# Low parts of the attention probabilities ahead of the low parts of the queries and keys in GpSimd's order, and a reciprocal inside the rope's products in VectorE's

## The reference

```
x: 4 x 512 x 256, xn = layernorm(x)
q = xn @ Wq (16 heads of 128), k = xn @ Wk, v = xn @ Wv (4 heads each, shared by 4 query heads)
q, k = rope with a scale by position; scores = q k^T / sqrt(128), causal; attn = softmax(scores)
s = (attn @ v) @ Wo
g = silu(MoE(xn)): 16 routed experts of width 176, top 2 by softmax, and a shared one of width 352
out = x + s * g
```

## Time and profile before

| | |
|---|---|
| median of 3 runs | 750.87 us (749.21 to 753.45) |
| the profiled execution | 753.45 us, its span 751.6 us |
| busy TensorE, VectorE, ScalarE, GpSimd | 628.6, 521.0, 498.9, 528.0 us |
| share of the span | 84%, 69%, 66%, 70% |
| mean granted clock of TensorE | 0.958 of full speed |
| rotate_lo on GpSimd, 80 of them | busy 92.2 us, idle ahead of them 100.0 us |
| low_probs on GpSimd, 64 of them | busy 167.2 us, idle ahead of them 3.9 us |

### The profile page before, as it was taken

The page is one execution under the profiler, slowest core; times in us unless marked ns, Lnnn a source line. Parts: engine busy times, 40 slices in busy tenths (PEclk is TensorE's granted clock), DMA queues, the critical chain, the costliest instruction groups (busy, mean ns, idle before and its releaser), DMA issues.

```text
span 751.6 us, 16683 instructions
## 1 busy us (share of the span) xinstructions
PE 628.6 (84%) x4610; PEld 421.9 (56%) x4611; DVE 521.0 (69%) x1555; ACT 498.9 (66%) x1333; POOL 528.0 (70%) x396
## 2 busy tenths in 40 slices
PE   3667849797989999899998999989877699999982
PEld 1244526464556566565665666656555477777761
DVE  5966649767788877888778887788845254333378
ACT  3685546757768787687867878678775665555542
POOL 4565567897886878878888787888988893554410
PEclk9878998999999999999999999999998899999996
DMA  9355973447544545444454444554486774655873
GB/s 301 93 127 120 211 184 64 90 75 166 101 84 87 97 88 103 86 87 92 89 103 90 87 88 89 102 96 89 85 135 169 211 132 87 147 140 135 215 266 106
DMA packets 233016, 92.39 MB, mean 123 GB/s; under 512 B 203316, under 2 KB 226324, under 8 KB 232980
## 3 DMA queue, kind: packets, MB, share of 16 engines
q1 hardware_dynamic: 228868, 81.40, 50.8%
q0 software_dynamic: 3840, 10.52, 4.7%
q10 hardware_dynamic: 272, 0.02, 0.0%
HBM read 24.72 MB, written 18.96 MB: 58 GB/s over the span
## 4 chain that ended last, share of the span: by engine, by line
POOL 41%; issue 27%; PE 16%; DVE 7%; DMA 5%; ACT 2%; SPq 1%; POOLq 1%; DVEq 0%; ACTq 0%
POOL stage L590 15%; POOL arena L574 11%; PE bank L1606 8%; POOL arena L581 6%; PE bank L1636 5%; POOL xs_dram L636 3%; POOL compare L632 2%; DMA stage<-w_down 2%; PE bank L1615 2%; DMA arena<-x 1%; POOL arena L566 1%; DMA ys_dram<-arena,row_u 1%; DMA arena<-ys_dram 1%; DVE s_sb L1333 1%; DVE arena L1148 1%
## 5 line engine op out<-in xcount | busy, mean ns | idle before, releaser
L830 ACT ACTIVATE arena<-bank,nmax 128x384 f32<-128x384 f32 (+2 forms) x320 | 146.8, 474 | 48.1 <-DVE nmax L1163 47.9
L590 POOL TENSOR_TENSOR stage<-arena,stage 128x1280 bf16<-128x1280 f32 x64 | 167.2, 2613 | 3.9 <-ACT stage L850 3.9
L581 POOL TENSOR_TENSOR arena<-arena 128x512 bf16<-128x512 f32 x80 | 92.2, 1159 | 100.0 <-ACT arena L815 99.8
L1458 PE MATMUL bank<-arena 128*128 128x512 f16 (+7 forms) x768 | 119.1, 306 | 22.0 <-POOL arena L581 19.9
L1163 DVE CUSTOM_DVE_ANT_0 bank<-bank,mask_b 128x512 f32<-128x512 f32 (+3 forms) x256 | 118.8, 519 | 17.8 <-issue 17.8
L1427 PE MATMUL bank<-xnT_hi,arena 128*128 (+1 forms) x320 | 114.1, 399 | 14.9 <-DVE arena L1148 9.7
L1472 PE MATMUL bank<-arena 128*128 128x512 f16 (+7 forms) x768 | 115.3, 300 | 0.0
L1498 PE MATMUL bank<-arena 128*128 (+2 forms) x768 | 99.8, 278 | 16.0 <-DVE arena L1154 13.2
L574 POOL TENSOR_TENSOR arena<-arena 128x512 f32<-128x512 f32 x77 | 98.2, 1284 | 10.3 <-DVE arena L1148 10.0
L1458 PEld LDWEIGHTS bank<-arena 128*128 128x128 f16 (+1 forms) x768 | 66.4, 100 | 65.5 <-issue 26.4
L1498 PEld LDWEIGHTS bank<-arena 128*128 (+2 forms) x768 | 75.5, 99 | 42.8 <-issue 17.6
(11 more groups left out here) (149 smaller groups left out, 1208.9 us busy)
## 6 DMA issues: line engine op xcount, KB each, us to landing
xs_dram<-s_sb SPq DMA_DIRECT2D x12, 516.0 KB, 5.0
stage<-w_gate_up SPq DMA_DIRECT2D x16, 352.0 KB
arena<-ys_dram SPq DMA_DIRECT2D x8, 512.0 KB, 8.4
stage<-w_down SPq DMA_DIRECT2D x16, 176.0 KB
stage<-wq SPq DMA_DIRECT2D x4, 512.0 KB, 7.6
stage<-wo SPq DMA_DIRECT2D x4, 512.0 KB, 7.6
arena<-stage SPq DMA_TRANSPOSE x128, 3.4
stage<-x SPq DMA_DIRECT2D x1, 2048.0 KB, 11.3
```

The source lines that it names most:

```text
L581: pool.tensor_tensor(dst, rot_a[buf], hi, ALU.subtract).then_inc(rot_lo, 1)
L590: pool.tensor_tensor(p_lo[par], probs[par], p_hi, ALU.subtract).then_inc(probs_lo, 1)
L830: return act.activation(dst, src, ACT.Exp, scale=-1.0, bias=nmax[:, par, qt:qt + 1], accum_out=rsum[:, par, to:to + 1])
L1458: ins = pe.matmul(score_bank[u][:, col:col + n_k], qT[a][:, j * S + qt * P:j * S + (qt + 1) * P], kT[m][:, 0:n_k], start=(n == 0), stop=(n ...
```

## The change

Nothing is computed otherwise. In GpSimd's order low_probs of a step comes ahead of the step's rotate_lo (in step 2 also ahead of rotate_sum of k), rotate_lo of k moves from step 2 to behind the steps, and behind the steps low_probs of head 4 comes ahead of rotate_lo of q2. In VectorE's rotate_products the reciprocal of a head's sums comes behind the first of the three products instead of behind the third.

```
--- before.py
+++ after.py
@@ -707,6 +707,7 @@
                     if j == 1 and rd.tile() is not None and not rd.last:
                         pool.wait_ge(rows_ready, rd.tile() + 1)
                         rows_low(rd.tile())
+                    low_probs(rd, j + 1)
                     if j == 2 and not rd.last:
                         rotate_sum("k", rd.item("k"))
                     if j == 1 and rd.tile() is not None and not rd.last:
@@ -715,9 +716,6 @@
                         rotate_lo("q3", rd.i * 5 + 5)
                     elif not rd.last:
                         rotate_lo(f"q{j - 1}", rd.rot(f"q{j - 1}"))
-                    if j == 2 and not rd.last:
-                        rotate_lo("k", rd.rot("k"))
-                    low_probs(rd, j + 1)
                     if rd.early and j < 2:
                         weights_lo(W_FIRST + 2 * rd.i + j)
                     if rd.last and j == 0:
@@ -737,11 +735,12 @@
                     if j == 1 and rd.tile() is not None and not rd.last:
                         scatter()
                 if not rd.last:
+                    rotate_lo("k", rd.rot("k"))
                     rotate_sum("q2", rd.item("q2"))
                     if rd.late:
                         shared_lo(1)
+                    low_probs(rd, GH)
                     rotate_lo("q2", rd.rot("q2"))
-                    low_probs(rd, GH)
 
             round_(Round(0, "first"))
             round_(Round(1, "second"))
@@ -1144,10 +1143,10 @@
                     dve.wait_ge(rot_lo, freed)
                 dve.tensor_tensor(rot_a[buf], ps[:], tab[:, cos, :], ALU.mult)
                 half = DH // 2
+                if inverted_head is not None:
+                    invert_sums(*inverted_head)
                 dve.tensor_tensor(rot_b[buf][0:half, :], ps[half:DH, :], tab[half:DH, sin, :], ALU.mult)
                 dve.tensor_tensor(rot_b[buf][half:DH, :], ps[0:half, :], tab[0:half, sin, :], ALU.mult).then_inc(misc_free, 1)
-                if inverted_head is not None:
-                    invert_sums(*inverted_head)
 
             def value_lo(rd):
                 dve.wait_ge(v_hi, rd.i + 1)
```

## The result

The changed kernel takes 777.8 us (median of 4 runs, 776.3 to 781.6); the kernel before took 750.04 beside it. The ratio is 1.037, with a 95% interval of 1.032 to 1.043: slower by 28 us. The range of the prediction held it because it was wide enough for a rival: the likeliest case, A (767, chance 0.57), did not happen, and rival B (778, chance 0.2) did. The profiled execution took 778.42 us with a span of 776.6, 25.0 over the span of before.

The account below looks back on a forecast made before the run. No engine is full; a ring of dependences across engines sets 31.45 us a round. -3.2 us ahead of the loop, +17.0 over eleven periods and +2.5 behind give +16.3: 767.2 us median, range 757 to 780.

Parts of the forecast that it names:

- A: Whole kernel: each loop round grows by 1.55 us with TensorE's clock kept; 767.2 us, chance 0.57.
- rival B: TensorE: wait ahead of head 4's score grows to about 2.4 us, clock falls every round; 778 us, chance 0.2.
- Part 1: GpSimd, step 2: low_probs of head 3 ahead of k's rotations costs 2.6 us a round before head 4's score.
- Part 2: GpSimd, step 1: low_probs of head 2 ahead of rotate_lo of q0 gains 1.0 us a round.
- Part 3: GpSimd, steps 3 and 0: low_probs of heads 4 and 1 earlier gain 0.1 of 0.67 us; q0's late rope eats the rest.
- Part 4: VectorE: the earlier reciprocal waits 1.0 us at q1, about 0.5 at q3 and k; counted 0 a round, to +0.5.
- The clock: TensorE ahead of head 4's score: likeliest forecast kept full clock, as a 2.4 us wait stays under 2.8; fall given 0.2.
- A's ring: Loop: cycle of dependences from one score of head 4 to the next, 33.05 us against 31.45, without a clock fall.
- B's price: Half-speed score takes 3.2 instead of 1.6 us; ScalarE's last unit starts 0.95 later, 12 x 0.95 = 11 us.
- Ahead of the loop: Rounds before the loop: earlier transfers and less idle time outweigh later losses; -3.2 us at rotate_sum of q1, round 3.
- Behind the loop: Round 14, behind the eleven periods: its rotate_lo of k still comes late, +2.5 us.

Follow-up runs that it names:

- part 2 alone: The kernel before with only low_probs of head 2 moved ahead of rotate_lo of q0; 742.7 us, ratio 0.988.
- part 4 alone: The kernel before with only the reciprocal moved behind the first product of each rope; 754.6 us, ratio 1.005.
- part 1 alone: The kernel before with only low_probs of head 3 moved ahead of rotate_sum of k and rotate_lo of q1 and k; 797.2 us, ratio 1.062.
- the filled kernel: The changed kernel with 8 useless matmuls added each round in TensorE's wait ahead of the score of head 4; 768.5 us, ratio 1.023.

## Why the prediction came out as it did

- *Part 1* (low3 ahead of RL k): forecast 7.55 us from RS q1 to the score; measured 354.54 to 361.96, 7.42. Right. Alone it makes the slowest kernel of all, and without it and part 4 the rest is a gain.
- *Part 2*: forecast 3.84 us from P2's end to the scatter's start and 1.0 us of gain; 0.90 alone. Right.
- *Part 3*: forecast 0.1 us of gain because the rope of q0 comes late; 0.06 alone. The first product waits for GpSimd as forecast.
- *Part 4*: forecast a wait of 1.0 us at q1 and 0.5 at q3 and k; alone it has 1.18, 0.49 and 0.49, and 1.18 at q0, which the working left out. Nothing in the loop, as forecast; ahead of the loop I had priced it at 0.5 us, and alone it costs 1.7 there and 0.5% of the time in all.
- *The clock is the step that failed.* A's ring of 33.05 holds TensorE at its upper level; the period is 34.03 with the clock fallen and 32.86 with it kept. The forecast weighed the fall as rival B at 0.2, with "2.4 is near 2.8" and "it is not reached". Two things were wrong in that. The 2.4 has no working beside it, and the idle time is longer: 3.12 us ahead of the score with the reciprocal in its old place, and in the changed kernel 2.04 us there and 1.24 us ahead of q2's projection, which part 4 makes and which ends 4.8 us before the other begins. And the length of a wait does not decide alone. These rows are, from the changed kernel, the score of head 4 in rounds 3, 13 and 14; from part 2 alone, that of round 14; and a score in round 1 from part 4 alone and from part 1 alone:

```profile
191.79 3.08 PE L1457 MATMUL bank<-arena 128*128 128x512 f16 x12 [2.12 <-POOL arena L581]
...
532.15 2.14 PE L1457 MATMUL bank<-arena 128*128 128x512 f16 x12 [2.05 <-POOL arena L581]
...
566.13 1.79 PE L1457 MATMUL bank<-arena 128*128 128x512 f16 x12 [2.37 <-POOL arena L581]
...
529.42 2.49 PE L1461 MATMUL bank<-arena 128*128 128x512 f16 x12 [1.99 <-POOL arena L581]
...
97.06 2.93 PE L1458 MATMUL bank<-arena 128*128 128x512 f16 x12 [2.58 <-ACT arena L830]
...
93.16 1.98 PE L1461 MATMUL bank<-arena 128*128 128x512 f16 x12 [2.58 <-ACT arena L833]
```

The third has the longest wait of the changed kernel's loop, 2.37 us, and the clock was kept (1.00, score 1.79). The fourth has a single wait of 1.99 us, with none over 0.4 in the 22 us ahead of it, and the clock fell (0.54 over 530.10 to 533.40). The last two have the same wait of 2.58 us: in one the clock fell and in the other it was kept. So a second wait is not needed for a fall, and what decides between like waits these runs leave open. By the Trainium skill (TensorE: Matmul & The Clock Gate, "HAM oscillation") a kernel with a wait ahead of every tile starts each tile cold. The trace agrees in that the clock fell at the wait in 11 of the 12 loop rounds. It differs in that the score starts at the upper level (0.96 over 327.93 to 328.73) and only then runs at the lower (0.50 over 328.73 to 332.10).
- *B's price* was right in sum and wrong in its way: 0.95 forecast; 0.98 over A's ring, and 1.17 over the filled kernel's. (The working put a score at 1.6 us, where the earlier trace rows has 1.80.) I let the slow score delay ScalarE's last unit and through it P4. P4 starts 4.27 us behind the score in the kernel before. In the changed kernel it is 5.01 in round 4, 4.72 in the round shown and 4.27, not late at all, in the round from 498.10, since the clock falls later and later into the score; E1 starts 8.26 or 8.27 us behind the score in all three, and the period is the same. So the cost does not come by P4. It comes through q3: its projection also runs at half speed, VectorE waits for it at the first product (0.99 us, row 332.83), and E1 starts at 8.27, in the filled kernel at 7.17. Here it is E1 that moves the ring. The way that I had forecast does show with the reciprocal put back: there P4 starts 5.40 us behind the score, and q0's first product waits 1.44 us for RL q2.
- *Ahead of the loop*: forecast -3.2 us at RS q1 of round 3; 184.36 against 187.41, -3.05. The transpose behind the fills was the cause named, and its wait is gone. That the sum fits so well is luck in part: at RS q1 of round 1 it was -6.1 where the working has -5.1, and the losses behind it came to 3.1 instead of 1.9.
- *Behind the loop*: forecast +2.5; from RS q1 of round 14 to the end it is 217.85 us against 218.02. The last round took it back. The step that failed is that I looked for no other wait there that would shrink. The traces have one: ScalarE waits for a weight load (w_down) ahead of a cast with the copy of the reciprocals behind it, 3.24 us before and 0.25 now, and TensorE's wait for that copy falls from 5.68 to 2.69 us. No run took this wait alone. Before, and after:

```profile
561.32 1.30 ACT L900 CAST arena<-stage 128x704 f16<-128x704 f32 x2 [3.24 <-DMA stage<-w_down]
...
585.97 1.30 ACT L899 CAST arena<-stage 128x704 f16<-128x704 f32 x2 [0.25 <-DMA stage<-w_down]
```

The sum in the profiles: -3.05 + 11 x 2.565 - 0.17 = +25.0 us, of which 11 x 0.98 = 10.8 is the clock over A. Two small slips of the working do not change this: it took 1.55 us a round where its ring gives 1.60, and it priced the clock for 12 rounds where the loop has 11 periods.

## What to carry to other kernels

In an order written by hand, follow the ring and ask of each move what it puts between two instructions on it. Here 2.6 us of work behind the instruction that TensorE waited for was off the ring, and ahead of it they cost their whole length. One rule for all steps (low parts of the probabilities first) hid that loss in the one step where the rotations were awaited, so measure the parts alone before giving up the whole. And when a change makes TensorE's waits longer, work out each wait, price the work behind it at the lower clock too, down to the next engine that needs it, and look at several rounds: one round does not show where the clock falls in the others.

## What the runs showed of the hardware that was not expected

The clock fell behind waits of about 2 us, and a wait's length did not settle it: it fell with 1.99 us (part 2 alone, round 14), with 2.03 to 2.12 (changed kernel, rounds 3 to 13) and with 2.58 (part 4 alone, round 1), and it was kept with 2.37 (changed kernel, round 14) and with 2.58 (part 1 alone, round 1). In the loop of the kernel before it was kept with all waits, the longest 1.70. Each fall in the changed kernel's loop came after TensorE had resumed, 0.3 us into the score in round 3 and 1.3 in round 13. Eight matmuls whose result is thrown away, 1.9 us of them in each round, made the kernel 9.3 us faster (777.8 to 768.5).
